# A grouped expert MLP with layer norm and rotation: another order of TensorE's two products, a second set of transposed rows, and new lists for the other engines

## The reference

```python
h = gelu(einsum('bsh,bhi->bsi', x, Wi[e]) + bi[e])      # 512 -> 2048, exact Gelu
o = einsum('bsi,bih->bsh', h, Wo[e]) + bo[e]            # 2048 -> 512
r = o + x
y = (r - mean(r)) * rsqrt(var(r) + 1e-12)
y = y * gamma[e] + beta[e]
# then, over groups of four columns, with theta and phi of the sequence:
out = [ y0*ct + y1*st, -y0*st + y1*ct, y2*cp + y3*sp, -y2*sp + y3*cp ]
```

## Time and profile before

| | us |
|---|---|
| median of three runs | 2757.75 |
| the profiled execution | 2766.84 |
| its span, first to last instruction | 2765.0 |
| PE busy | 2677.4 (97%) |
| VectorE busy | 1956.6 (71%) |
| ScalarE busy | 936.3 (34%) |
| GpSimd busy | 1319.9 (48%) |
| mean granted TensorE clock | 0.994 |

### The profile page before, as it was taken

The page is one execution under the profiler, slowest core; times in us unless marked ns, Lnnn a source line. Parts: engine busy times, 40 slices in busy tenths (PEclk is TensorE's granted clock), DMA queues, the critical chain, the costliest instruction groups (busy, mean ns, idle before and its releaser), DMA issues.

```text
span 2765.0 us, 54858 instructions
## 1 busy us (share of the span) xinstructions
PE 2677.4 (97%) x12310; PEld 1208.9 (44%) x12311; DVE 1956.6 (71%) x4931; ACT 936.3 (34%) x1697; POOL 1319.9 (48%) x1560
## 2 busy tenths in 40 slices
PE   5999999999999999999999999999999999999998
PEld 2444444444444444444444444444444444444443
DVE  5677777676777776776777776767767776677776
ACT  6333333333333333333333333333333333333332
POOL 0687447860037870677500577607873677500000
PEclk9999999999999999999999999999999999999999
DMA  6766655855455855668644658646665657444343
GB/s 187 187 152 153 154 149 129 182 136 103 87 133 135 184 133 114 170 122 178 140 91 90 159 120 184 144 92 167 166 157 128 172 121 179 111 97 87 83 96 65
DMA packets 741351, 375.98 MB, mean 136 GB/s; under 512 B 682816, under 2 KB 682944, under 8 KB 732608
## 3 DMA queue, kind: packets, MB, share of 16 engines
q1 hardware_dynamic: 677136, 173.16, 35.9%
q0 software_dynamic: 27312, 135.28, 15.2%
q10 hardware_dynamic: 36864, 67.13, 7.9%
HBM read 174.13 MB, written 33.55 MB: 75 GB/s over the span
## 4 chain that ended last, share of the span: by engine, by line
PE 81%; DMA 6%; DVE 5%; issue 4%; DVEq 2%; ACT 2%; ACTq 0%; SPq 0%; POOLq 0%; POOL 0%
PE z_ps L833 41%; PE o_ps L842 40%; DMA xT<-x 3%; DMA xbuf<-in_x 2%; DVE z_ps L641 1%; DMA hT<-h 1%; DVEq L197 1%; ACT z_ps L444 1%; DVE h L651 0%; ACT x L439 0%; DMA wi<-in_L_cond_Wi 0%; ACTq L197 0%; DVE y L696 0%; DVE ln L668 0%; DVE r_ps L667 0%
## 5 line engine op out<-in xcount | busy, mean ns | idle before, releaser
L833 PE MATMUL z_ps<-wi,xT 128*128 x6096 | 1406.5, 381 | 32.3 <-issue 16.1
L842 PE MATMUL o_ps<-wo,hT 128*128 (+1 forms) x6144 | 1410.7, 379 | 10.8 <-DMA hT<-h 10.8
L833 PEld LDWEIGHTS z_ps<-wi,xT 128*128 128x128 f16 x6096 | 598.0, 98 | 763.1 <-issue 61.2
L842 PEld LDWEIGHTS o_ps<-wo,hT 128*128 128x128 f16 x6144 | 601.8, 98 | 739.8 <-issue 19.8
L444 ACT ACTIVATE z_ps<-z_ps 128x512 f32<-128x512 f32 x512 | 299.5, 585 | 1732.3 <-DVE z_ps L641 1727.9
L641 DVE SCALAR_TENSOR_TENSOR z_ps<-z_ps,tok,bi_all 128x512 f32<-128x512 f32 x512 | 387.2, 757 | 195.2 <-PE z_ps L833 133.1
L378 POOL TENSOR_TENSOR wi<-staged 128x512 f32<-128x512 f32 x112 | 118.5, 1058 | 658.1 <-DVE r_ps L661 647.0
L651 DVE SCALAR_TENSOR_TENSOR h<-z_ps,tok,h 128x512 f16<-128x512 f32 x512 | 380.2, 743 | 10.0 <-ACT h L450 9.5
L450 ACT ACTIVATE h<-z_ps,tok 128x512 f16<-128x512 f32 x512 | 351.9, 687 | 19.0
L646 DVE SCALAR_TENSOR_TENSOR x<-xbuf,tok,x 128x512 f16<-128x512 f16 (+1 forms) x128 | 117.2, 916 | 185.8 <-ACT x L439 185.8
L696 DVE SCALAR_TENSOR_TENSOR y<-r_ps,rot,y 128x128 f32<-128x128 f32 x512 | 194.5, 454 | 5.2 <-ACT y L457 2.0
(11 more groups left out here) (126 smaller groups left out, 1366.9 us busy)
## 6 DMA issues: line engine op xcount, KB each, us to landing
staged<-in_L_cond_Wi POOLq DMA_DIRECT2D x56, 1024.0 KB, 5.9
staged<-in_L_cond_Wo POOLq DMA_DIRECT2D x56, 1024.0 KB, 6.6
xbuf<-in_x ACTq DMA_DIRECT2D x128, 256.0 KB, 3.3
out<-y ACTq DMA_DIRECT2D x128, 256.0 KB, 3.4
hT<-h SPq DMA_TRANSPOSE x512, 4.1
bi_all<-in_L_cond_bi POOLq DMA_DIRECT2D x7, 1024.0 KB, 8.3
wi<-in_L_cond_Wi SPq DMA_DIRECT2D x4, 1024.0 KB, 8.5
wo<-in_L_cond_Wo POOLq DMA_DIRECT2D x4, 1024.0 KB, 5.9
```

The source lines that it names most:

```text
L833: last = t.matmul(z_ps[:, n, :], xT16[:, j, a, k, :], wi16[:, bass.ds(b, 1), w, k, cs], start=(k == 0 and (a, w) == PASSES[0]), stop=(k == ...
L842: last = t.matmul(o_ps[:, j, :], hT16[:, n, a, c, :], wo16[:, bass.ds(b, 1), w, n * GC + c, :], start=(n == 0 and c == 0 and (a, w) == PAS ...
```

## The change

TensorE takes all four banks of the first product of s, and then all four groups of the second product of s - 1. `hT16` gets a second set, chosen by k, and the semaphore `s_bg2` goes. SyncE's list in a slot becomes: x of s + 1, then the four banks of h of s. ScalarE's begins with the high part of x of s + 1, the load of x of s + 2 and the store of s - 3; the four Gelus follow, with the wait for x's transpose (now of the next slot) before the fourth, then `turn_own` and `sum_x`. VectorE's has the low part of x before bank 0, does the low part of bank 3 in its own slot, and normalises between bank 2 and bank 3.

```diff
-        hT16 = sb("hT16", [P, NB, 2, GC, P], F16)
+        hT16 = sb("hT16", [P, 2, NB, 2, GC, P], F16)
...
             def iteration(s, k, inner=False):          # SyncE
-                if there(s, -1, inner):
-                    transpose_h(NB - 1)
                 if there(s, 1, inner):
                     transpose_x(1 - k)
                 if there(s, 0, inner):
-                    for n in range(NB - 1):
-                        if not inner and s == 1:
-                            sp.wait_ge(s_bg2, n + 1)
-                        transpose_h(n)
+                    for n in range(NB):
+                        transpose_h(n, k)
...
                 if ahead:                              # ScalarE
-                    act.wait_ge(s_xT, (s + 1) * 16)
-                if here:
-                    gelu_bank(s, k, 0)
-                if ahead:
                     hi_x(s + 1)
+                if there(s, 2, inner):
+                    fetch_x(s + 2, k)
                 if there(s, -3, inner):
                     store(s - 3)
                 if here:
+                    gelu_bank(s, k, 0)
                     gelu_bank(s, k, 1)
-                if there(s, 2, inner):
-                    fetch_x(s + 2, k)
+                    gelu_bank(s, k, 2)
                 if there(s, -3, inner):
                     act.wait_ge(s_y, (s - 2) * 16)
+                if inner or 1 <= s < S - 2:
+                    act.wait_ge(s_xT, (s + 2) * 16)
                 if here:
-                    gelu_bank(s, k, 2)
+                    gelu_bank(s, k, 3)
...
                     scale_h(s, k, b)                   # VectorE
-                    z_bank(s, 0, b)
-                if back and (inner or s > 1):
-                    lo_group(s - 1, 1 - k, NB - 1)
                 if ahead:
                     lo_x(s + 1)
+                if here:
+                    z_bank(s, 0, b)
                 if last:
                     moments(s - 2, b2)
...
                     root()
-                    normalise(s - 2, b2)
                 if here:
                     z_bank(s, 2, b)
                     lo_group(s, k, 1)
+                if last:
+                    normalise(s - 2, b2)
+                if here:
                     z_bank(s, 3, b)
                     lo_group(s, k, 2)
+                    lo_group(s, k, 3)
...
-                for n in range(NB):                    # TensorE
-                    if here:
+                    for n in range(NB):
                         first_product(s, k, n, b)
-                    if back and n == 0:
-                        pe.wait_ge(s_wo, r1 + 1)
-                        if inner or s >= 3:
-                            pe.wait_ge(s_res, s - 2)
-                    if back:
+                if back:
+                    pe.wait_ge(s_wo, r1 + 1)
+                    if inner or s >= 3:
+                        pe.wait_ge(s_res, s - 2)
+                    for n in range(NB):
                         second_product(s - 1, 1 - k, n, b1)
```

More of the change, by code:

```diff
@@ L127, in expert_mlp_rotate_kernel @@
         boot_ps = pb("boot_ps", [P, BANK])
-        hid = hT16[:].rearrange("p n a c t -> p (n a c t)").bitcast(F32)
+        hid = hT16[:, 0].rearrange("p n a c t -> p (n a c t)").bitcast(F32)
         keys_i = hid[:, 0:129].bitcast(I32)
@@ L164, in expert_mlp_rotate_kernel @@
         s_blo = sem("s_blo")
-        s_bg2 = sem("s_bg2")
         s_bias = [sem(f"s_bias{i}") for i in range(2)]
@@ L251, in transpose_x, with transpose_h @@
                                        x16[:].rearrange("p a n -> p (a n)")).then_inc(s_xT, 16)
-            def transpose_h(n):
+            def transpose_h(n, k):
                 sp.wait_ge(s_hlo[n], 1)
                 sp.sem_clear(s_hlo[n])
-                sp.dma_start_transpose(hT16[:, n].rearrange("p a c t -> p (a c) t"),
+                sp.dma_start_transpose(hT16[:, k, n].rearrange("p a c t -> p (a c) t"),
                                        h16[:, n].rearrange("p a t -> p (a t)")).then_inc(s_hT[n], 16)
             def iteration(s, k, inner=False):
-                if there(s, -1, inner):
-                    transpose_h(NB - 1)
                 if there(s, 1, inner):
@@ L487, in iteration @@
                     turn_own(s - 2)
-                if here:
-                    gelu_bank(s, k, 3)
                 if there(s, 2, inner):
@@ L703, in iteration @@
                 ahead, here = inner or 2 <= s < S - 1, there(s, 0, inner)
-                back, last = there(s, -1, inner), there(s, -2, inner)
+                last = there(s, -2, inner)
                 b = r = b2 = None
@@ L788, in _ @@
             iteration(0, 0)
-            lo_group(0, 0, NB - 1)
             scale_x(2)
@@ L841, in second_product @@
                     for a, w in PASSES:
-                        last = t.matmul(o_ps[:, j, :], hT16[:, n, a, c, :], wo16[:, bass.ds(b, 1), w, n * GC + c, :],
+                        last = t.matmul(o_ps[:, j, :], hT16[:, j, n, a, c, :], wo16[:, bass.ds(b, 1), w, n * GC + c, :],
                                         start=(n == 0 and c == 0 and (a, w) == PASSES[0]),
@@ L846, in second_product @@
                     last.then_inc(s_g2, 1)
-                return last
             def iteration(s, k, inner=False):
@@ L857, in iteration @@
                     pe.wait_ge(s_wi, r + 1)
-                for n in range(NB):
-                    if here:
+                    for n in range(NB):
                         first_product(s, k, n, b)
-                    if back and n == 0:
-                        pe.wait_ge(s_wo, r1 + 1)
-                        if inner or s >= 3:
-                            pe.wait_ge(s_res, s - 2)
-                    if back:
+                if back:
[3 more added lines that the diff above has]
+                    for n in range(NB):
                         second_product(s - 1, 1 - k, n, b1)
@@ L876, in first_iteration @@
                     pe.wait_ge(s_blo, Q + n + 1)
-                    last = second_product(0, 0, n, 0)
-                    if n < NB - 1:
-                        last.then_inc(s_bg2, 1)
+                    second_product(0, 0, n, 0)
             def column_sums(m):
```

## The result

The changed kernel took **2729.9 us** (median of five runs, 2728.93 to 2733.71), against 2757.75 before: a ratio of 0.9893, 95% interval 0.9869 to 0.9916. The forecast was 2723 us. So 28 us went where 35 were forecast, 1.0% and not 1.3%. The profiled execution took 2733.55 us with a span of 2731.5 and a mean granted clock of 0.996.

What follows compares the result with a forecast made beforehand. PE, busy 97%, was taken as the bound, losing 47.1 us mainly to late transposes. 2765.0 - 47.1 + 1.0 (start) + 2.0 (leftovers) = 2720.9 us of span; with 1.84 more, 2723 us; range 2712 to 2745.

Steps and rivals of the forecast that it cites:

- the 47.1 us: PE's loss from the third sequence on: waits for transposed x and h, "issue" waits, and matmuls at the lower clock.
- the 16.1: PE's 21 waits called "issue", 16.1 us in all; the prediction counted the long ones as late transposes too.
- the undisturbed body: One pass of the four-sequence loop without late transposes: mean 83.24 us, four times 20.7 and 0.4 at the jump back.
- What makes the transposes late: In an undisturbed sequence x's transpose leaves 8.6 in, due at 20.7; h's first leaves 11.9 in, due at 23.3.
- h's later due times: PE's new order makes h's banks due at 31.1 to 38.9 us instead of 23.3 to 38.9.
- Leftovers: Term of 2 us added for transposes that still come late in the changed kernel.
- the start's due time: At the start, four groups come first, so the third sequence's transpose is due at 84.3; gain 5.29 + 1.96 us.
- the first rival: Full DMA engines make transposes late, so leaving earlier only moves waits: 2741 or 2761 us; chance 0.15.
- the 16.7 and 21.9: Times allowed in the new lists: 16.7 us for x's transpose, at least 21.9 for h's last bank.
- the second rival: VectorE becomes the bound if waits add over 2.9 us a turn, 0.9 counted; 2860 us at 4.0; chance 0.06.
- The third rival: Late transposes don't cause PE's "issue" waits; about 12 us and two low-clock groups, 3.6, stay: 2739 us; chance 0.07.

Runs made afterwards that it cites:

- e3: Kernel before with only x's part early (load, high part, low part, transpose); TensorE's order and single set of rows kept: 2724.26 us, ratio 0.9877.
- e9: Kernel before with two of TensorE's four table reads moved behind the first bank's matmuls: 2760.78 us, ratio 0.9994.
- e2: Changed kernel with TensorE's order alone undone, bank and group alternating again: 2727.32 us, ratio 0.9895.
- e10: Kernel before with the edits of e3 and e9 together: 2715.81 us, ratio 0.983.
- e4: Changed kernel with two of the four table reads of PE's sequencer moved from the head of the sequence to between the two products: 2710.72 us, ratio 0.983.
- e5: Kernel before without GpSimd's 1 MB weight loads after the first two, its arithmetic kept: 2729.82 us, ratio 0.9873.
- e11: Changed kernel with bn_stats five times instead of once, 2.93 us more VectorE work a sequence: 2980.68 us, ratio 1.0791.
- e1: Changed kernel with x's part of the lists put back to its late places on VectorE and ScalarE: 2917.74 us, ratio 1.0581.
- e6: Changed kernel without GpSimd's 1 MB weight loads after the first two, its arithmetic kept: 2723.89 us, ratio 0.9859.
- e12: e1 with VectorE's two table reads for the sequence moved behind the residual: 2921.7 us, ratio 1.0579.
- e8: Kernel before with x's high part, low part and transpose early, the load of x left in place: 2728.95 us, ratio 0.9871.
- e7: Kernel before with only the load of x moved to the head of ScalarE's list: 2737.9 us, ratio 0.9912.

## Why the prediction came out as it did

**Where the 47.1 us came from: right.** They were late transposes, most of "issue" included (e3, e9); e9 leaves at most 7 us to the two reads themselves. In the prediction's list of names the 16.1 holds some 4.2 us in sixteen short waits, of 0.15 to 0.35 each, which the undisturbed body has as well; five long ones make 11.9. The 47.1 does not depend on it.

**What makes the transposes late: right for x, and too narrow.** The prediction compared an undisturbed departure with the due time. The loaded sequence shows more. In the kernel before, the load of x issued at 491.49 landed 11.28 later; then VectorE:

```profile
503.58 0.15 DVE L619 TENSOR_SCALAR tok<-tok 128x1 int32<-128x1 int32 x1 [4.70 <-ACT boot_ps L433]
...
510.50 0.86 DVE L646 SCALAR_TENSOR_TENSOR x<-xbuf,tok,x 128x512 f16<-128x512 f16 x1 [1.44 <-ACT x L439]
```

and SyncE:

```profile
511.45 5.23 SPq L250 DMA_TRANSPOSE xT<-x  x1
516.79 14.76 SPq L257 DMA_TRANSPOSE hT<-h  x4
```

PE began this sequence at 498.93. A late load holds VectorE's first instruction for 4.70 us, and what stands behind it leaves later: x's transpose at +12.5 instead of the 8.6 of the earlier trace rows, h's first at +17.9 instead of 11.9. In e3, whose PE begins the same sequence at 498.70, h's first leaves at +10.5 (SyncE's timeline from 509 to 525 us):

```profile
509.19 11.45 SPq L257 DMA_TRANSPOSE hT<-h  x3
```

So moving x's part mends h as well.

**TensorE's order: the step that was mis-credited.** The prediction let h's later due times (31.1 to 38.9) remove h's waits. e2 and e3 keep the old due times and have 3.5 and 2.8 us of them; h's waits went because h leaves earlier. TensorE's order and the second set are worth about 4 us, at the start (e10). Since the change holds both parts, the sum did not suffer; that it held is luck here, since the step named the wrong part.

**Leftovers: the mis-sized term.** 2.0 forecast, 12.5 found. I gave the start's due time for the first bank alone (84.3). The fourth leaves with the row at 74.05 and was needed at 93.1:

```profile
74.05 8.35 SPq L256 DMA_TRANSPOSE hT<-h  x4
```

It released PE at 93.47. PE's sequencer, held there, had lost its lead: its four reads begin at 94.7 and the last at 97.9, while the twelve matmuls in hand end at 96.23, so PE stood 3.02 us and then ran at the low clock. In the loop the reads alone cost some 7 us, beside the 10.4 that the body already held. The prediction had seen the mechanism in the earlier trace rows but tied it to late transposes only; e4 shows that it needs none. The reads of PE's sequencer in the changed kernel (ns, min/median/max):

```profile
L196 PEldq TENSOR_LOAD <-tab x508: 294/308/1234, 49.3 to 2705.9; - x170
```

Four at the median, with the register work between them, about fill the lead that PE leaves; one of 1 us does not fit.

**Bandwidth, the first rival: fell.** PE is busy 19.83 and 19.89 of 20 us at shares of 0.89 and 0.97. Beside the loads transposes stay long: the longest of x's takes 10.9 us and of h's 16.0 (13.8 and 12.0 before; the prediction had put h's at 12 at most), within the 16.7 and 21.9 that the prediction gave them. The Trainium skill says in "DMA: Bandwidth & Descriptors", section "Issuing engines are not separate DMA queues", that DMAs of all issuers run on the same 16 engines and interleave. The runs do not contradict it: the stretch moved 241 GB/s after and 240 before. With the lists of before these loads make transposes late (e5); with the lead of the new ones PE doesn't notice.

**VectorE, the second rival: did not happen, but was nearer than stated.** It was to decide from 2.9 us of added waits, with 0.9 counted, so 2.0 to spare; 0.9 was to spare (e11). Not foreseen was `L612 <- issue`, 1.09 us a sequence (135.7 / 125), against 13.4 us in 15 for the same instruction before: the reads in front of it now stand bare. Why they were covered before is not shown. e1, with 2.1 us a sequence at the low part, is over the edge.

**The third rival: half right.** It kept 12 us of "issue", and the changed kernel has 12.0 us of it, which is chance: these are 29 waits at heads of sequences, all but the one at 99.25 with nothing late before them, and not the five long ones behind late transposes; and in the kernel before these waits were not a cost apart from the late transposes (e9). With the transposes in time the reads are what is left, and moving two of them is worth 17 to 19 us (e4).

**Open:** why one table read now and then takes 1 us instead of 0.3 (the loads have a part in it at most: without them, in e6, the slowest of PE's takes 897 ns instead of 1234, and "issue" is 5.5 us instead of 12.0); what VectorE's bare reads cost (e12); and why the copy of x's low part takes up to 2.9 us in the changed kernel, at a median of 0.77. That the kernel before stays 6 us above the changed one without loads (e5, e6) is no riddle: of e5's waits 4.0 us are the start's, and the rest in its loop meets the bias loads.

## What to carry to other kernels

When a consumer waits for late data, look first at what the producer's turn began with and what held it: here the places of x's load, high part, low part and transpose in three lists, toward the head of the turn, gave nearly all that a new order and a second buffer were credited with. Move first steps of a chain toward the head of the list, where they buy lead: here the high and low part alone (e8) gave more than the load alone (e7). Measure the slack of the second busiest engine by adding work of known length: a visible wait can cover reads that come back when it is gone. And when an engine's queue runs dry at the same place each turn, look for what its sequencer does there, and put half of it elsewhere.

## Not expected of the hardware

A read of one table value from SBUF by PE's sequencer takes 294 to 1234 ns, median 308, far apart for the same instruction. The four at the head of a sequence, with what the sequencer does between them, take about as long as the matmuls that PE still has queued. Of the sequence at 2522.34 (ns as above, first and last start in us):

```profile
L196 PEldq TENSOR_LOAD <-tab x4: 298/298/668, 2518.6 to 2521.3; - x4
```

They begin at 2518.6, the last at 2521.3, and PE ran dry at 2522.17, 0.17 us before its next matmul: a cover of some 3.6 us, which four reads just overrun and two (e4) do not.
